# Transposes in the banks of the y products, and a group's output scaled and added by VectorE

## The reference

```python
x = x + 0.5 * _L0_ffn_ref(_layernorm(x), ...)   # a product plus 8 low-rank experts, top 2
x = x + _L0_attn_ref(_layernorm(x), ...)        # 32 heads of 16, 8 key heads
x = x + 0.5 * _L0_ffn_ref(_layernorm(x), ...)
x = x + 0.5 * _L1_ffn_ref(_layernorm(x), ...)   # SwiGLU, 1376 wide
x = x + _L1_attn_ref(_layernorm(x), ...)        # Mamba2: the part that is changed
x = x + 0.5 * _L1_ffn_ref(_layernorm(x), ...)
```

```python
yg = y * silu(gate)
rstd = rsqrt(mean(square(yg), over the group's 1024 channels) + EPS)
out = (yg * rstd) * norm_w
return out @ out_proj_w.T
```

## Time and profile before

| | before |
|---|---|
| time of three runs, median (lowest to highest) | 2431.77 us (2427.7 to 2436.87) |
| the profiled execution: its time, its span | 2418.28 us, 2416.2 us |
| Mamba2 steps, in the profile | 650 to 2205 us |
| mean granted clock of TensorE | 0.97 of full speed |

### The profile page before, as it was taken

The page is one execution under the profiler, slowest core; times in us unless marked ns, Lnnn a source line. Parts: engine busy times, 40 slices in busy tenths (PEclk is TensorE's granted clock), DMA queues, the critical chain, the costliest instruction groups (busy, mean ns, idle before and its releaser), DMA issues. The chain is left out here.

```text
span 2416.2 us, 38770 instructions
## 1 busy us (share of the span) xinstructions
PE 2192.4 (91%) x12539; PEld 1762.2 (73%) x12554; DVE 1708.9 (71%) x2632; ACT 1440.4 (60%) x3106; POOL 1088.8 (45%) x814
## 2 busy tenths in 40 slices
PE   6879979997799989989989999998998999896999
PEld 5756567886677767777777777777776777774887
DVE  7767765132688878878878877886987887886221
ACT  2267723333677677677776667766767676762332
POOL 4366534443145354454344434434435443544442
PEclk9899999999899999999999999999999999997999
DMA  3000012331332223223322322222332233220332
GB/s 122 1 1 1 1 40 57 94 94 44 127 105 101 90 108 114 79 80 132 114 80 79 131 89 93 100 79 91 125 110 80 96 119 106 83 101 23 94 94 83
DMA packets 62568, 203.01 MB, mean 84 GB/s; under 512 B 6928, under 2 KB 6928, under 8 KB 53904
## 3 DMA queue, kind: packets, MB, share of 16 engines
q1 hardware_dynamic: 62352, 200.31, 24.6%
HBM read 197.39 MB, written 2.88 MB: 83 GB/s over the span
## 5 line engine op out<-in xcount | busy, mean ns | idle before, releaser
L480 POOL TENSOR_TENSOR wAl<-rawA,wAh 128x512 fp32r<-128x512 f32 x233 | 314.5, 1360 | 413.9 <-ACT wAh L608 412.9
L1396 PE MATMUL ps<-xTh,wAh 128*128 128x512 f32 x1512 | 433.5, 409 | 50.6 <-DVE work L1235 25.8
L1235 DVE SCALAR_TENSOR_TENSOR work<-ps,chp,work 128x510 f32<-128x510 f32 (+2 forms) x480 | 353.8, 744 | 93.2 <-ACT work L784 66.3
L1396 PE MATMUL ps<-xTl,wAh 128*128 128x512 f32 x1512 | 419.1, 400 | 0.0
L1396 PE MATMUL ps<-xTh,wAl 128*128 128x512 f32 x1512 | 415.3, 397 | 0.0
L1396 PEld LDWEIGHTS ps<-xTh,wAh 128*128 128x128 f32 x1512 | 279.3, 191 | 127.6 <-DVE work L1235 31.7
L1396 PEld LDWEIGHTS ps<-xTl,wAh 128*128 128x128 f32 x1512 | 288.8, 191 | 69.6
L1396 PEld LDWEIGHTS ps<-xTh,wAl 128*128 128x128 f32 x1512 | 285.9, 189 | 68.9
L818 ACT ACTIVATE eb<-eb,gc 128x128 f32<-128x128 f32 x1024 | 312.5, 391 | 14.8 <-DMA eb<-scr_decays 14.8
L486 POOL TENSOR_TENSOR wBl<-rawB,wBh 128x512 fp32r<-128x512 f32 x108 | 139.1, 1300 | 344.0 <-ACT wBh L612 344.0
L784 ACT ACTIVATE work<-ps,gpar 128x512 f32<-128x512 f32 x160 | 121.2, 767 | 190.4 <-PE ps L1396 183.6
(11 more groups left out here) (185 smaller groups left out, 4032.9 us busy)
## 6 DMA issues: line engine op xcount, KB each, us to landing
eb<-scr_decays SPq DMA_DIRECT2D x64, 1536.0 KB, 6.4
rawA<-ma_in SPq DMA_DIRECT2D x144, 256.0 KB, 3.7
rawA<-fa_in SPq DMA_DIRECT2D x88, 256.0 KB, 2.7
rawB<-mb_in SPq DMA_DIRECT2D x64, 256.0 KB, 2.8
rawB<-fb_in SPq DMA_DIRECT2D x44, 256.0 KB, 2.7
x<-x_in SPq DMA_DIRECT2D x8, 256.0 KB, 6.6
x_out<-x SPq DMA_DIRECT2D x8, 256.0 KB, 2.7
wqraw<-wqkv_in SPq DMA_DIRECT2D x1, 1536.0 KB, 10.9
```

Of the source, the lines that this page charges most:

```text
L480: nc.gpsimd.tensor_tensor(wAl[:, slot, :], rawA[:, slot, :], wAh[:, slot, :].bitcast(F32), ALU.subtract).then_inc(A_lo, 1)
L1235: nc.vector.scalar_tensor_tensor(out=acc[:, :, j:S], in0=src[:, :, 0:S - j], scalar=param(g, c // 2, 3 - j), in1=acc[:, :, j:S], op0=ALU.m ...
L1396: return nc.tensor.matmul(o, l, r, start=start, stop=end, **kw)
```

## The change

1. `TBANK` becomes 5 and 6, the banks of the y products. The transposes then wait for the skip that empties these banks (`m_yx`), and no longer for the emptying of the transposes before and for the output sums. The output products of t = 1 and 2 no longer wait for `scale_x` (`m_xdt`), but for the sums of the tiles before. The products C B^T go to banks 3 and 4 (`CBANK`).
2. `scale_out` on ACT and `add_out` on POOL (56 instructions each) are dropped. DVE does both in one instruction, `update` (`x = oacc * rstd + x`), just before it overwrites that tile of `oacc`: that is in steps 1 and 2 of the next group, ahead of each of the eight evacuations.
3. In even steps DVE evacuates t = 4 between the first and the second tap of the second convolved chunk, and no longer after both chunks' taps.
4. In step 7 ACT does the first SiLU and the third `conv_start` before the second half of `spans`, and so on through the six convolved chunks.
5. DVE's loop now goes from step 3 to step 2 of the next group: steps 1 and 2 of the first group, which have no update, stand ahead of it.

```diff
-    TBANK = (3, 4)
+    TBANK = YBANK
+    CBANK = (3, 4)
...
-        def add_out(g, t):
-            pool.wait_ge(m_scaled, NT * g + t + 1)
-            pool.wait_ge(x_new, XB[4] + NT * (g + 1))
-            nc.gpsimd.tensor_tensor(x[:, t, :], x[:, t, :], oacc[:, t, :], ALU.add).then_inc(x_new, 1)
...
-        def scale_out(g, t):
-            act.wait_ge(m_rstd, g + 1 + FREE)
-            act.wait_ge(m_osum, 32 * g + 24 + t + 1 + FREE)
-            nc.scalar.activation(oacc[:, t, :], oacc[:, t, :], ACT.Copy,
-                                 scale=rstd[:, t:t + 1]).then_inc(m_scaled, 1)
...
+            if len(conv) > 2:
+                conv_silu(gn, conv[0])
+                conv_start(gn, conv[2], slot)
+                conv_silu(gn, conv[1])
+                conv_start(gn, conv[3], slot)
+                y_hi(g, v, 0)
+                y_hi(g, v, 1)
+                conv_silu(gn, conv[2])
+                conv_start(gn, conv[4], slot)
+                conv_silu(gn, conv[3])
+                conv_start(gn, conv[5], slot)
+                spans(*vn, 1)
+                conv_silu(gn, conv[4])
+                conv_silu(gn, conv[5])
...
+        def update(g, t):
+            if t % 4 == 0:
+                dve.wait_ge(m_rstd, g + 1 + FREE)
+            dve.wait_ge(m_osum, 32 * g + 24 + t + 1 + FREE)
+            nc.vector.scalar_tensor_tensor(out=x[:, t, :], in0=oacc[:, t, :], scalar=rstd[:, t:t + 1],
+                                           in1=x[:, t, :], op0=ALU.mult, op1=ALU.add).then_inc(x_new, 1)
...
             if j == 0:
-                dve.wait_ge(x_new, g * NT + XB[4] + t + 1)
+                if not (isinstance(g, int) and g == 0):
+                    update(g - 1, t)
+                    dve.wait_ge(x_new, g * NT + XB[4] + t + 1)
...
             if more:
                 taps(gn, conv[0])
-                taps(gn, conv[1])
-            if v % 2 == 0 and not first:
-                for t in range(4, NT):
-                    evacuate(*((v - 1, g) if v else (TPG - 1, g - 1)), t)
+                taps(gn, conv[1], (1,))
+                if drain:
+                    evacuate(*before, 4)
+                taps(gn, conv[1], (2, 3))
+            if drain:
+                for t in range(5, NT):
+                    evacuate(*before, t)
...
             if not (isinstance(k, int) and k == 0):
-                pe.wait_ge(m_xdt, 2 * k + p - 1)
-                if v % 2 == 1:
-                    pe.wait_ge(m_osum, 32 * g + 8 * (v // 2) + FREE)
-                if v == 1:
-                    pe.wait_ge(m_var, g + FREE)
+                pe.wait_ge(m_yx, 2 * k + p - 1 + FREE)
...
-                elif t in (1, 2) and not edge:
-                    pe.wait_ge(m_xdt, 2 * (k + 1) + t)
                 elif t in (1, 2):
                     pe.wait_ge(m_osum, 32 * g + 8 * j + FREE)
+                    if v == 1 and t == 2:
+                        pe.wait_ge(m_var, g + FREE)
+                    if v == TPG - 1 and not end:
+                        pe.wait_ge(m_cbm, B * (g + 2))
```

More of the change, by code:

```diff
@@ L577, in _ @@
             step(0, g + 1)
-            step1_adds(g)
             step(1, g + 1)
@@ L873, in step @@
                 hi_A(A0G + i, g, NA_G)
[L874 to L887, removed]
+            if len(conv) > 2:
[12 more added lines that the diff above has]
+                conv_silu(gn, conv[5])
+            else:
+                spans(*vn, 1)
+                conv_silu(gn, conv[0])
+                conv_silu(gn, conv[1])
+                y_hi(g, v, 0)
             gate_silu(gn, gate[0])
@@ L1223, in conv_index, with taps @@
             return g * XCH + (c if tile < 2 else 4 + (tile - 2) // 2 * 2 + c % 2)
-        def taps(g, c):
+        def taps(g, c, which=(1, 2, 3)):
             n, k = conv_index(g, c), conv_index(0, c)
@@ L1229, in taps @@
             src = ps[:, c % 3, :].rearrange("p (b l) -> p b l", b=2)
-            for j in range(1, 4):
+            for j in which:
                 if j == 1:
@@ L1321, in step @@
             more = not (last and v == TPG - 1)
+            drain = v % 2 == 0 and not first
+            before = (v - 1, g) if v else (TPG - 1, g - 1)
             if more:
                 taps(gn, conv[0])
-                taps(gn, conv[1])
-            if v % 2 == 0 and not first:
-                for t in range(4, NT):
-                    evacuate(*((v - 1, g) if v else (TPG - 1, g - 1)), t)
+                taps(gn, conv[1], (1,))
[5 more added lines that the diff above has]
+                    evacuate(*before, t)
                 if v == 0:
@@ L1383, in _ @@
         step(0, 0, first=True)
+        step(1, 0)
+        step(2, 0)
         with dve.Fori(0, NG - 1) as g:
-            for v in range(1, TPG):
+            for v in range(3, TPG):
                 step(v, g)
-            step(0, g + 1)
-        for v in range(1, TPG):
+            for v in range(3):
+                step(v, g + 1)
+        for v in range(3, TPG):
             step(v, NG - 1, last=True)
@@ L1685, in y_products, with out_products @@
             last.then_inc(m_y, 1)
-        def out_products(v, g, half, edge=False):
+        def out_products(v, g, half, end=False):
             k, j = g * TPG + v, v // 2
```

26 lines of the change are left out of this document (6 added, 20 removed).

## The result

The changed kernel takes 2344.45 us (median of 4 runs, 2343.08 to 2348.62), the kernel before 2430.70 us run beside it: ratio 0.9645, 95% interval 0.9622 to 0.9668, so 3.55% or 86 us faster. The forecast was 2371, its range 2343 to 2404: the sign and the range held, the range by 1.5 us at its lower end, and the point was 27 us too high. The changed kernel's profiled execution took 2343.08 us, its span is 2341.3; the span before was 2416.2, so in the profiles the gain is 74.9 us.

A forecast was written before the change was run, and what follows sets the result against it. PE, busy 91% of the span, gains only where it waits. Steps 1 to 3 (29), 4 to 6 (15.6), 7 (18.2) and the first group (2.4) make 65 us, less clock 60: median 2371 us, range 2343 to 2404.

The forecast's parts named there:

- the `xo` waits: PE's output products: the bank change removes these waits, gaining 0.95 us in step 3, 0.85 in step 5, 0.7 in step 7.
- rival C: DVE never holds PE: 31 us more gain, less 5 for the clock, time 2343 us; chance 0.12.
- Steps 1 to 3: Lengths 21.5, 23.2 and 22.5 us, sum 67.2 against 71.3: gain 4.1 us a group, 29 us in all.
- Steps 4 to 6: Evacuation and `xo` waits go: 0.63 + 0.85 + 0.63 = 2.1 us a group, 15.6 us with the last group's 0.9.
- The clock: Low clock at the start of step 1 follows PE's loop wait, which stays: three times 1.7 us taken back.
- The median: Median of the runs before lay 13.5 us above the profiled execution; forecast for the median 2431.8 - 60.8 = 2371 us.
- Step 7: ACT's earlier `conv_start` and the banks remove 1.9 + 0.7 = 2.6 us of PE's waits, 18.2 us in all; step at 34.6.
- A: Odd steps: the wait only moves from the second product to the fourth; 17.5 us not gained, time 2389; chance 0.13.
- B: Contended updates and an uncovered DVE jump eat the 29 us of steps 1 to 3: time 2400; chance 0.17.
- D: DVE becomes the bound of the group, so the kernel is slower: two us above the limit give 2446; chance 0.06.
- E: The change does nothing, each wait removed being followed at once by the next: time 2432; chance 0.05.
- The loop's jump on DVE: DVE's moved jump is covered by two decays and costs nothing; 1.4 us a group if only the last covers it.

The follow-up runs named there:

- b_banks: Kernel before with only the bank change (transposes in the y products' banks, C.B products in banks 3 and 4, PE's waits with them): 2382.20 us, ratio 0.9823.
- b_act7: Kernel before with only the order of ACT's step 7 changed: 2411.93 us, ratio 0.9939.
- b_evac4: Kernel before with only the evacuation of t = 4 moved between the taps: 2407.14 us, ratio 0.9920.
- b_update: Kernel before with only the update of x as one DVE instruction and DVE's loop jump moved behind step 2: 2413.08 us, ratio 0.9943.
- a_noupd: Changed kernel with the update of x as before (ACT's scale_out, POOL's add, DVE's loop jump at step 1): 2350.83 us, ratio 0.9695.
- e_hint: Changed kernel with the eight updates put where DVE idles in steps 0 and 1, plus a hint for PE's loop branch: 2318.77 us, ratio 0.9561.
- m_hint: Changed kernel with the updates spread over steps 0 to 2, plus a hint for PE's loop branch: 2304.79 us, ratio 0.9492.
- m_plain: Changed kernel with the updates spread over steps 0 to 2, without a hint for PE's loop branch: 2323.50 us, ratio 0.9560.

## Why the prediction was right, and where it was off

**Sign and range.** The places were right: the `xo` waits, ACT's late `conv_start` in step 7, the evacuation of t = 4, and ACT's `scale_out`s ahead of step 1 did hold PE, and b_banks, b_act7, b_evac4 and b_update show each by itself. The range held narrowly, and its lower end by a slip: it is rival C's time, given as 2343, but C's own terms, 31 less 5, make 2345.

**Steps 1 to 3: the sum right by luck, its division and its cause not.** Forecast 21.5 + 23.2 + 22.5 = 67.2; measured 21.2 + 24.9 + 21.3 = 67.3. The wait in step 2 is where the prediction put it, ahead of t = 7. But 2.0 of the measured 67.3 are clock, which the forecast's three terms do not hold: two of seven step 1s are at 0.92 (22.17 against 20.68 us), and all six step 2s inside the loop are at 0.93, 1.5 us each. At full clock the three are about 20.7 + 23.3 + 21.3 = 65.3, so step 2 was met, step 1 was 0.8 us too long in the forecast and step 3 1.2 us, and the clock made up for it. (Step 1's 21.5 does not follow from its own terms either: 20.9 + 0.2 + 0.75 is 21.85.) The failed step is the one that gave the 29 us to the update, but for the 0.95 us a group of the banks in step 3: a_noupd has all of them without the update. The prediction never worked out what the banks do in step 1 alone; that was 3.1 us a group.

**Steps 4 to 6: mis-sized.** Forecast 0.63 + 0.85 + 0.63 = 2.1 a group, measured 0.91 + 1.15 + 0.94 = 3.0. The failed step is "a step without waits takes about 20.9 us when odd and 20.7 when even": it subtracted the idle times that the profile shows, and each wait costs 0.3 us more. Steps without waits take 20.6 and 20.4. Over seven groups that is 6 us, and in the first group's steps 1 to 3 another 1.5 (3.9 measured, 2.4 forecast). Steps 0 and 7 together came out within 2 us.

**The clock: counted beside the sum.** I took back 5 us for low stretches behind the jump. The stretches were there and cost more, 12 us over the groups in steps 1 and 2, as worked out above, mostly in step 2, where the prediction had none. But the measured 67.3 us hold them already, so beside these sums the 5 us are part of the miss.

**The median: 12 us.** The forecast added the 13.5 us by which the runs of before stood above their profiled execution. For the changed kernel the same difference was 1.4 us. The ten runs of the kernel before beside the last three kernels went from 2420.64 us at a mean granted clock of 0.971 to 2440.38 at 0.962; 0.9% of some 2190 us of PE's work is those 20 us. So the offset is within what the clock makes of runs of one kernel. The profiled execution, at 0.970, was at the fast end of them (others at 0.970 took 2418.74 and 2424.95 us), and its distance from a median is no part of the kernel. These terms (6, 1.5, 5 and 12) are 24.5 of the 27 us missed.

**What was to be seen.** The waits for `xo` are gone, step 1 is under 23 us in every group; its clock is above 0.95 in five of seven. Step 2 has its wait for `oacc`. Step 3 has almost no idle time for the decay (0.2 us a group, where 1.1 to 1.4 were reckoned), though with 21.3 us it is 0.7 above a step without waits. Step 7 came to 35.1 us on average, not 34.6.

**The rivals.** A: wrong in steps 3, 5 and 7 (no recorded wait is left at the fourth product there), right in step 1 of a kernel where ACT is still late. B: the updates were 0.74 us where POOL was idle, and 0.80 to 1.9 beside it; the worst case did not come, but in steps 1 to 3 they did eat what they gained, as a_noupd shows. C came nearest to the measured time, but its mechanism is not what happened: DVE does hold PE, for 18.1 us. D and E: no. The loop's jump on DVE cost nothing, as taken; decays and updates both cover it.

## What to carry to other kernels

A wait that is taken away is worth what the next one behind it leaves, so price each part on top of the others and not only alone: here the update took 6.4 us out of step 1 of the old kernel and put 4.4 back into step 2, and the hint on PE's jump was worth nothing with one order of DVE's updates (e_hint) and 19 us with another (m_hint beside m_plain). When work moves onto the engine that feeds the bound one, put it where that engine idles and not where the data is first touched: the same eight instructions cost 20 to 24 us less there. In this kernel PE's recorded idle time understated short waits by about 0.3 us, and a wait of that size did not show: compare the starts of like matmuls. And look at the clock of a step before its length is explained by waits: steps of this kernel differ by 1.5 us between 1.00 and 0.92 to 0.96.

## What was not expected of the hardware

- **A wait costs PE 0.3 us beyond its recorded idle time.** Steps with recorded waits of 0.61, 0.88 and 0.64 us became shorter by 0.91, 1.15 and 0.94 when the waits went, and one with none by 0.31.
- **The jump at the end of PE's loop** took its sequencer 5.5 us and left PE idle for 15.8 us in all over the six times that it is taken, with one instruction transfer inside each; with a hint at the loop's top it took 0.36 us, and this wait is gone.
- **The same update took 737 to 1885 ns.** DVE's timeline of the changed kernel, beside POOL's weight split and squares, and then alone:

```profile
1239.14 1.89 DVE L1280 SCALAR_TENSOR_TENSOR x<-oacc,rstd,x 128x512 f32<-128x512 f32 x1
1241.06 0.69 DVE L1292 COPY oacc<-ps 128x512 f32<-128x512 f32 x1
...
1254.65 0.74 DVE L1280 SCALAR_TENSOR_TENSOR x<-oacc,rstd,x 128x512 f32<-128x512 f32 x1
```

  The copy between them, from PSUM, is 0.69 us in either place. That POOL's work is the cause is read from the coincidence (POOL splits weights from 1239.17 us for 3.00 us) and was not tried by itself. The coincidence is a close one: in each of the seven groups four updates took 737 to 745 ns, with POOL idle or beside them for 0.1 us at most, and the four beside its work 804 to 1885 ns.
- **Runs of one kernel differ by 0.8% with the granted clock** (0.962 to 0.971, 2440 to 2421 us), which is as much as one part of this change is worth.
